# Table words of several target sets or edge units taken by one register load in a graph network kernel

## The chip, the cores and the metric

The kernel runs on one core of a Trainium2 chip. The metric is the device time of one execution in microseconds; of several runs the median counts.

## The reference, cut to what matters

There are 3125 nodes with 128 features and 100000 edges, sorted by target. Four graph layers follow each other, each with a residual sum and a layer norm: an edge MLP with batch norm, a two-way graph convolution, a residual network of four steps, and attention over the edges.

```python
edge_index = jnp.stack([src, dst])
x = _layernorm(x + _L0_gnn_ref(x, edge_index, ...), axis=-1)
x = _layernorm(x + _L1_gnn_ref(x, edge_index, ...), axis=-1)
x = _layernorm(x + _L2_gnn_ref(x, edge_index, ..., 4), axis=-1)
x = _layernorm(x + _L3_gnn_ref(x, edge_index, ...), axis=-1)

def _L0_gnn_ref(x, edge_index, W1, b1, g1, be1, W2, b2, g2, be2):
    edge_features = jnp.concatenate([x[src], x[dst]], axis=1)
    h = jax.nn.relu(_batchnorm(edge_features @ W1.T + b1, g1, be1))
    edge_updates = jax.nn.relu(_batchnorm(h @ W2.T + b2, g2, be2))
    return jax.ops.segment_sum(edge_updates, dst, num_segments=x.shape[0])
```

The other three layers need, for every pair of nodes, how many edges join them: the kernel counts that first, in a matrix, and then works with the matrix in place of the edges.

## The kernel before, in words

All five engines run their own instruction streams, written out by hand, and meet at the ends of stages. Three stages are of interest here.

**Counting (79 to 840 us).** The padded 3200 nodes are cut into NWIN = 100 sets of WN = 32 targets. The edges are taken in pairs of 128, 392 in all (NPAIR). A set's edges lie in a run of pairs, from `first` to `end`, at least two of them; neighbours may share a pair. For each pair VectorE (`one_hots`, L1392 on) makes two one-hot tiles of the sources (L1397) and one of the targets (L1399), in one of eight slots (PAIRS); TensorE (`count_pair`) multiplies them into PSUM (L1752), with four matmuls. A set ends with a matmul on zeros (L1791) that tells the others. Each engine loops on its own over the sets, VectorE in groups of four (`count_four`), TensorE in groups of twelve (GROUP, `count_group`), and for each set it needs three numbers: `first`, `end` and `before`, which with a pair's number gives its place in the run of all visits and so its slot and semaphore value. They come from a table in SBUF, `block_tab`, made by VectorE in the preparation (L1353 to L1365); row 3 holds first and end in one word, row 2 `before`. `window` (L393) reads them by `value_load`, one load per word, each with an assertion on its bounds. `before` is loaded only for the first set of a group; otherwise it is worked out in registers from the set ahead (L401). In this stage GpSimd gathers rows of a table for the first pass by indirect DMAs (L823), held back by the counts of VectorE (`one_ready`) and later by the ends of sets (`window_done`); ScalarE takes the counts out of PSUM and stores them.

**First pass over the edges (975 to 1515 us).** 98 units (NU) of 1024 edges. TensorE (`layer1`) adds the gathered source rows (L1886) and, for each block of 128 target nodes that the unit touches, a product with a one-hot tile (L1892) made by VectorE (`pass1`, L1506); then follows `layer2`, two f32 matmuls (L1905). Three of four units' rows come through DRAM (`a_in`), the fourth is gathered straight into SBUF (`a_direct`).

**Second pass (1515 to 2045 us).** The same units again. `layer2_rows` recomputes the second layer: two matmuls for the shift (L1938), 16 in f32 (L1940). ScalarE (`relu2`, L1109) and VectorE (`low_part`, L1539) take the high and low part; VectorE makes one-hot rows (L1549); `sum_edges` multiplies them, 16 matmuls per visit of a block (L1953), ScalarE (`take_sums`, L1120) takes the sum out and GpSimd (`add_sums`, L905) adds it to the node's sum. TensorE's loop takes two units per round: rows(i,0), sums of unit 2i-1, rows(i,1), sums of unit 2i.

In both passes the numbers of a unit come by `unit` (L383): one load (L386) of one packed word of `unit_tab`, with its bounds step and assertion, and then masks and shifts (L388). On each engine the load stands directly ahead of the loop over the unit's blocks.

The numbers are register values of an engine's sequencer, which also waits for semaphores, works out addresses and hands instructions to its engine.

Of the kernel before, what the change touches and what calls it, by code (L numbers as in the profile page):

```python
# [21 lines left out]
P = 128  # L22
N = 3125
NB = -(-N // P)
# [7 lines left out]
NU = EP // UE  # L32
PE_EDGES = 256
NPAIR = EP // PE_EDGES
WP = 98
WN = 32
NWIN = NP // WN
# [49 lines left out]
PAIR0 = 512  # L87
VISIT0 = 64
PAIRS = 8
SETS = 3  # L90
GROUP = 12
# [10 lines left out]
def gnn(nc, ins, out):  # L102
# [28 lines left out]
    with ctx:  # L131
# [53 lines left out]
        unit_tab = sb("unit_tab", [1, 4, NU], i32)  # L185
        block_tab = sb("block_tab", [1, 4, NWIN], i32)
        parts_tab = sb("parts_tab", [1, 8], i32)
# [4 lines left out]
        weff = sb("weff", [P, P], f32)  # L192
        wtmp = sb("wtmp", [P, 4, P], f32)
        squares = sb("squares", [P, 2 * P], f32)
# [187 lines left out]

        def unit(eng, g):  # L383


            word = eng.value_load(unit_tab[0:1, 3, ds(g, 1)], min_val=0, max_val=(VISIT0 + NB * NU) * 1024)  # L386
            def number(value, least, most):
                return nc.s_assert_within(eng.snap(value), least, most)  # L388

            return (number(word & 31, 0, NB - 1), number((word >> 5) & 31, 1, NB),  # L390
                    number(word >> 10, 0, VISIT0 + NB * NU))

        def window(eng, w, done_pairs):  # L393
# [384 lines left out]
        def _(pool):  # L778
# [113 lines left out]
            for n in range(4, 7):  # L892
                stage_start("pool", pool)
                if n == 4:

                    pool.wait_ge(S["bn2_ready"], 1)
                    pool.sem_inc(S["agg_added"], VISIT0)

                    def add_sums(i):
                        for s in range(2):  # L900
                            first, end, before = unit(pool, 2 * i + s)
# [28 lines left out]
        def _(act):  # L930
# [182 lines left out]

            def take_sums(i, s):

                first, end, before = unit(act, 2 * i + s)
# [7 lines left out]
            relu2(0, 1)  # L1124
            take_sums(0, 0)
            with act.Fori(1, NU // 2 - 1) as i:
                relu2(i, 0)
                take_sums(i + -1, 1)
                relu2(i, 1)
                take_sums(i, 0)  # L1130
            relu2(NU // 2 - 1, 0, False)
            take_sums(NU // 2 - 2, 1)
            relu2(NU // 2 - 1, 1, False)
            take_sums(NU // 2 - 1, 0)
            take_sums(NU // 2 - 1, 1)
            norm_act(act)
# [115 lines left out]
        def _(dve):  # L1252
            v = nc.vector

            def do(i):
                stepped("dve", dve, i)
# [148 lines left out]
            def count_four(i):  # L1405
                done_pairs = None
                for q in range(4):
                    w = 4 * i + q
                    first, end, before = window(dve, w, done_pairs)
# [87 lines left out]

            def pass1(j, q):
                i = 2 * j + q
                for s in range(2):  # L1500
                    g = 2 * i + s
                    first, end, before = unit(dve, g)
# [12 lines left out]
            dve.sem_inc(S["visit_ready"], VISIT0)  # L1515
            pass1(0, 0)
            with dve.Fori(0, NU // 4) as j:
                pass1(j, 1)
                pass1(j + 1, 0)
            count(NU - 2, NU - 2, 0)  # L1520
# [20 lines left out]

            def one_hot_rows(i, s):

                g = 2 * i + s
                first, end, before = unit(dve, g)
                low_part(i, s)
# [7 lines left out]

            def pass2(i):
                for s in range(2):
                    one_hot_rows(i, s)

            pass2(0)
            with dve.Fori(1, NU // 2) as i:  # L1560
                pass2(i)
            first, end, before = unit(dve, NU - 1)
            dve.wait_ge(S["agg_added"], before + end)
# [162 lines left out]
        def _(pe):  # L1726
# [49 lines left out]
            def count_group(g, ms):  # L1776
                done_pairs = None
                for m in ms:
                    w = GROUP * g + m
                    known = isinstance(w, int)  # L1780
                    first, end, before = window(pe, w, done_pairs)
                    done_pairs = before + end
# [88 lines left out]

            def layer1(j, q, s, odd=0):
# [4 lines left out]
                first, end, before = unit(pe, 2 * i + s)  # L1877
                after(pe, S["r1_made"], 2 * i + s - 1)
# [29 lines left out]

            layer1(0, 0, 0)
            layer1(0, 0, 1)  # L1910
            layer2(0, 0)
            assert NU // 4 % AHEAD == 0
            with pe.Fori(0, NU // 4 // AHEAD) as jj:
                for odd in range(AHEAD):
                    j = AHEAD * jj + odd
                    for q in (1, 0):
                        i = 2 * j + (2 - q)
                        layer1(j + (1 - q), q, 0, odd)
                        layer2(i + -1, 1)
                        layer1(j + (1 - q), q, 1, odd)  # L1920
                        layer2(i, 0)
# [21 lines left out]

            def sum_edges(i, s):

                first, end, before = unit(pe, 2 * i + s)
                hold("pe", pe, S["low_ready"], 2 * i + s + 1)
# [14 lines left out]
            layer2_rows(0, 1)  # L1962
            sum_edges(0, 0)
# [5 lines left out]
            sum_edges(NU // 2 - 1, 1)  # L1969
            pe.wait_ge(S["dve_features"], 2)  # L1970
# [253 lines left out]
```

## Time and profile before, and how to read them

| | |
|---|---|
| median of 3 runs | 4250.56 us (4240.57 to 4261.32) |
| span of the profiled execution, first to last instruction | 4243.9 us |
| median less span | 6.7 us |
| PE busy | 3447.9 us, 81% |
| DVE busy | 2654.4 us, 63% |
| ACT busy | 1496.2 us, 35% |
| POOL busy | 1050.2 us, 25% |

The profiled execution has no time of its own beside its span. PE is the matmul engine, PEld its weight loads, DVE VectorE, ACT ScalarE, POOL GpSimd, SP SyncE. An engine's name with a q (DVEq, PEldq) marks instructions of its sequencer, which don't count as busy; PE's stand under PEldq. Idle time before an instruction is put down to the one whose semaphore released it, or to "issue" where nothing visible was waited for.

### The profile page before, as it was taken

The numbers are of one execution on the slowest core, as the hardware profiler recorded it, in microseconds if no ns is written. First come the engines' busy times: TensorE is split into PE (matmuls) and PEld (weight loads), VectorE is DVE, ScalarE is ACT, GpSimd is POOL, SyncE is SP. The second block draws the span as 40 slices with busy tenths as digits, with TensorE's granted clock in tenths as the row PEclk, the third lists the DMA queues.
The fourth block names the chain that finished last, engine by engine and source line by source line (L and its number), as shares of the span: only waits on it lengthen the run. The fifth ranks groups of instructions, "written<-read, shape, count | busy, mean of one in ns | idle before, by whom it ended". The sixth has DMA issues, their size and how long they took to land. (4 is left out here: it accounts for less than half of the span.)

```text
span 4243.9 us, 85956 instructions
## 1 busy us (share of the span) xinstructions
PE 3447.9 (81%) x20439; PEld 1689.6 (40%) x20548; DVE 2654.4 (63%) x3759; ACT 1496.2 (35%) x2093; POOL 1050.2 (25%) x1132
## 2 busy tenths in 40 slices
PE   3777767686677978888898998599889989989996
PEld 1333333243344556666645554233322233332223
DVE  6877766522233455554202223699989989989995
ACT  2134555601122222222202111221088851208883
POOL 3877774665555412221000001000010000000000
PEclk8989999978898999999899999799999999999998
DMA  2255665667787866666583774511054331103333
GB/s 62 93 168 196 213 224 193 222 248 255 240 276 253 304 214 200 179 175 171 187 276 130 246 257 143 148 61 54 23 140 132 115 116 54 62 16 128 117 123 73
DMA packets 373635, 688.38 MB, mean 162 GB/s; under 512 B 136131, under 2 KB 223297, under 8 KB 372769
## 3 DMA queue, kind: packets, MB, share of 16 engines
q1 hardware_dynamic: 236400, 361.19, 26.8%
q10 hardware_dynamic: 112052, 274.54, 18.8%
q0 software_dynamic: 25088, 51.43, 4.8%
q8 instruction: 54, 0.88, 0.1%
q14 instruction: 41, 0.34, 0.0%
HBM read 453.91 MB, written 208.37 MB: 156 GB/s over the span
## 5 line engine op out<-in xcount | busy, mean ns | idle before, releaser
L823 POOL DMA_INDIRECT gat<-a_table,gidx x592 | 674.3, 1139 | 259.3 <-issue 142.5
L1703 DVE SCALAR_TENSOR_TENSOR pw<-ex,c_full 128x1564 f32<-128x1564 f32 x400 | 680.8, 1779 | 35.6 <-ACT ex L1231 30.9
L1231 ACT ACTIVATE ex<-psum 128x782 f32<-128x782 f32 x800 | 610.4, 826 | 77.4 <-PE psum L2114 58.9
L1665 DVE CUSTOM_DVE_ANT_0 masked<-psum,masks 128x1784 bf16<-128x1784 f32 x320 | 551.7, 1784 | 64.8 <-ACT masks L1204 43.7
L1752 PE MATMUL psum<-one_src,one_dst 128*128 x1968 | 417.7, 351 | 208.9 <-DVE one_dst L1399 127.6
L1397 DVE TENSOR_SCALAR one_src<-iota_sub,src_low 128x800 f16 x984 | 382.6, 430 | 191.7 <-PE psum L1752 124.7
L2123 PE MATMUL psum<-pw,vaug 128*32 128x391 f32 x3200 | 348.6, 508 | 30.2 <-DVE pw L1703 10.0
L1752 PEld LDWEIGHTS psum<-one_src,one_dst 128*128 x1968 | 189.4, 100 | 422.9 <-issue 340.4
L1539 DVE SCALAR_TENSOR_TENSOR u<-psum,u 128x1024 f16<-128x1024 f32 x98 | 120.0, 1225 | 254.8 <-ACT u L1109 254.8
L1204 ACT ACTIVATE masks<-masks,far 128x3128 bf16<-128x3128 bf16 x40 | 115.5, 2900 | 423.4 <-DMA masks<-ct_parts 423.4
L1067 ACT ACTIVATE r<-psum,vec 128x1024 f32<-128x1024 f32 x98 | 118.0, 1205 | 398.7 <-PE psum L1898 331.4
L1399 DVE SCALAR_TENSOR_TENSOR one_dst<-row_c,window_at,iota_row 128x256 f16 x492 | 234.2, 476 | 0.0
L823 POOL DMA_INDIRECT a_direct<-a_table,gidx x192 | 184.4, 961 | 166.0 <-DMA a_direct<-a_table,gidx 98.5
L2079 PE MATMUL psum<-qp,kp 96*128 96x446 bf16 (+1 forms) x700 | 172.8, 364 | 60.8 <-DVE mx L1665 31.0
L905 POOL TENSOR_TENSOR y<-y,visit_sum 128x128 f32 x122 | 105.2, 862 | 455.5 <-ACT visit_sum L1120 455.5
L1940 PE MATMUL psum<-w2s,r_in 128*128 128x128 f32 x1568 | 217.6, 296 | 0.0
L1940 PEld LDWEIGHTS psum<-w2s,r_in 128*128 128x128 f32 x1568 | 198.0, 205 | 44.2 <-issue 44.2
L1953 PE MATMUL psum<-u,ohd 128*128 128x128 f16 x1952 | 147.7, 227 | 71.6 <-issue 35.5
L1506 DVE TENSOR_SCALAR oht<-dst_bc,nodec 128x1024 f16 x122 | 60.7, 498 | 224.4 <-PE psum L1892 123.8
L1905 PE MATMUL psum<-r,W2T 128*128 128x512 f32 x392 | 198.9, 631 | 0.0
L1494 DVE BATCH_NORM_STATS2 stats<-psum 128x512 f32 (+1 forms) x196 | 126.5, 687 | 108.0 <-PE psum L1905 107.8
L2084 PE MATMUL psum<-qp,kp 96*128 96x448 bf16 x800 | 189.4, 360 | 0.0
(357 smaller groups left out, 4792.0 us busy)
## 6 DMA issues: line engine op xcount, KB each, us to landing
c_full<-c_whole SPq DMA_DIRECT2D x80, 977.5 KB, 5.0
r_edges<-r ACTq DMA_DIRECT2D x98, 512.0 KB
r_in<-r_edges ACTq DMA_DIRECT2D x98, 512.0 KB, 3.7
c_ring<-ct_parts SPq DMA_DIRECT2D x100, 480.0 KB, 4.4
c_whole<-c_sum ACTq DMA_DIRECT2D x100, 400.0 KB
a_edges<-gat SPq DMA_DIRECT2D x148, 256.0 KB, 2.6
a_in<-a_edges ACTq DMA_DIRECT2D x74, 512.0 KB, 5.6
c_ring<-ct_parts SPq DMA_DIRECT2D x100, 320.0 KB, 3.6
```

What stands on the lines that cost most here:

```text
L823: g.indirect_dma_start(to, None, a_table, bass.IndirectOffsetOnAxis(ap=gidx[:, s, k:k + 1], axis=0)).then_inc(landed, 16)
L1231: a.activation(ex[:, step_slot(n // 2), (n % 2) * 2 * CW:(n % 2 + 1) * 2 * CW].rearrange("p (h t) -> p h t", h=2), psum[:, o:o + 2 * BANK] ...
L1397: v.tensor_scalar(one_src[:, ds(slot, 1), t, 0:SUB].rearrange("p o n -> p (o n)"), iota_sub[:, :], src_low[:, ds(p * 2 + t, 1)], None, ALU ...
L1399: v.scalar_tensor_tensor(one_dst[:, ds(slot, 1), :, :].rearrange("p o t n -> p (o t) n"), row_c[:, ds(p * 2, 2)].rearrange("p (t o) -> p t ...
L1665: v.tensor_tensor_reduce(out=masked[:, n % 2, 0:count * width].rearrange("p (c t) -> p c t", c=count), in0=psum[:, first * BANK:(first + c ...
L1703: v.scalar_tensor_tensor(pw[:, step_slot(k), :].rearrange("p (h t) -> p h t", h=HQ), ex[:, step_slot(k), :].rearrange("p (h t) -> p h t", ...
L1752: last = t.matmul(bank(2 * k + half, n), one_dst[:, ds(slot, 1), s, :].rearrange("p o n -> p (o n)"), one_src[:, ds(slot, 1), s, half * HA ...
L1905: last = t.matmul(bank(4 + 2 * s + half), W["W2T"][:, :], r1[:, s, half * GE:(half + 1) * GE], start=True, stop=True)
L1940: last = t.matmul(psum[:, s * UE + k * P:s * UE + (k + 1) * P], r1_in[:, s, k * P:(k + 1) * P], w2s[:, :], start=False, stop=True, skip_gr ...
L2079: last = t.matmul(bank(first + c, width), kp[0:KQK, n // 2, ds(b * P, P)], query(quad, n // 2)[0:KQK, c0 + c * width:c0 + (c + 1) * width] ...
L2084: t.matmul(bank(7, 448), kp[0:KQK, n // 2, 0:P], query(quad, n // 2)[0:KQK, 0:448], start=True, stop=True)
L2123: last = t.matmul(psum[hh * HW:(hh + 1) * HW, 6 * BANK:6 * BANK + CW], vaug[:, k, quad * HQ + hh, :], pw[:, step_slot(k), hh * CW:(hh + 1) ...
```

## The change

Words of several sets or units are read by one load on each engine. In the counting a new table `quad_tab` has a row of five words for each group of four sets: `before` of the first set and the packed first and end of each. In the passes 2 to 4 neighbouring words of `unit_tab` are read at once. Where the load now stands differs: at the head of the loop's round, ahead of `layer2_rows`, `relu2` or `layer1`, in place of behind them. TensorE now loads `before` for the first of every four sets, ahead only for the first of a group of twelve.

```diff
-        block_tab = sb("block_tab", [1, 4, NWIN], i32)
+        block_tab = sb("block_tab", [1, 3, NWIN], i32)
+        quad_tab = sb("quad_tab", [1, NWIN // 4, 5], i32)
...
-        wtmp = sb("wtmp", [P, 4, P], f32)
+        wtmp = sb("wtmp", [P, 2, P], f32)
...
-        def unit(eng, g):
-            word = eng.value_load(unit_tab[0:1, 3, ds(g, 1)], min_val=0, max_val=(VISIT0 + NB * NU) * 1024)
+        def unit_words(eng, g, n):
+            return nc.values_load_multi_w_load_instructions(
+                unit_tab[0:1, 3, ds(g, n)], engines=[eng.engine], min_val=0, max_val=(VISIT0 + NB * NU) * 1024)[1]
+        def unit(eng, word):
...
-        def window(eng, w, done_pairs):
-            word = eng.value_load(block_tab[0:1, 3, ds(w, 1)], min_val=0, max_val=NPAIR * 512 + NPAIR)
+        def quad_words(eng, i):
+            return nc.values_load_multi_w_load_instructions(
+                quad_tab[0:1, ds(i, 1), :].rearrange("p o n -> p (o n)"), engines=[eng.engine],
+                min_val=0, max_val=NPAIR * 512 + NPAIR)[1]
+        def window(eng, words, q, done_pairs):
+            word = words[1 + q]
             first = nc.s_assert_within(eng.snap(word & 511), 0, NPAIR - 2)
             end = nc.s_assert_within(eng.snap(word >> 9), 2, NPAIR)
-            if done_pairs is None:
-                before = eng.value_load(block_tab[0:1, 2, ds(w, 1)], min_val=PAIR0 - NPAIR, max_val=PAIR0 + NWIN * NPAIR)
-            else:
-                before = nc.s_assert_within(eng.snap((done_pairs - first) & 65535), PAIR0 - NPAIR, PAIR0 + NWIN * NPAIR)
+            before = words[0] if q == 0 else (done_pairs - first) & 65535
+            before = nc.s_assert_within(eng.snap(before), PAIR0 - NPAIR, PAIR0 + NWIN * NPAIR)
...
-            do(v.scalar_tensor_tensor(block_tab[:, 3, :], block_tab[:, 1, :], 512.0, block_tab[:, 0, :], ALU.mult, ALU.add))
+            by_quad = block_tab[:, :, :].rearrange("p a (g q) -> p a g q", q=4)
+            do(v.scalar_tensor_tensor(quad_tab[:, :, 1:5], by_quad[:, 1, :, :], 512.0, by_quad[:, 0, :, :], ALU.mult, ALU.add))
+            do(v.tensor_copy(quad_tab[:, :, 0:1], by_quad[:, 2, :, 0:1]))
...
             def count_four(i):
                 done_pairs = None
+                words = quad_words(dve, i)
...
             with pe.Fori(1, NU // 2) as i:
+                words = unit_words(pe, 2 * i + -1, 2)
                 layer2_rows(i, 0)
-                sum_edges(i + -1, 1)
+                sum_edges(i + -1, 1, words[0])
                 layer2_rows(i, 1)
-                sum_edges(i, 0)
+                sum_edges(i, 0, words[1])
```

The first pass is alike with four words per round on TensorE and VectorE; in the second VectorE and GpSimd load two words at the head of a pair of units, ScalarE two words ahead of `relu2`.

## Rows read from the trace of the kernel before

**Rows 1.** Busy us (and instructions) of each engine in the stages; PEclk is the granted clock.
```profile
core 0: us, PE busy (x) PEld busy (x) DVE busy (x) ACT busy (x) POOL busy (x), PEclk, DMA share, GB/s
79.00:840.00 761.00, 549.98 (x2656) 247.96 (x2656) 551.43 (x1478) 333.94 (x593) 547.42 (x544) 0.92 0.53 181
...
1515.00:2045.00 530.00, 433.18 (x3851) 339.21 (x3850) 265.84 (x224) 135.14 (x225) 105.15 (x122) 0.94 0.65 189
```
**Rows 2.** Who waited for whom, 79 to 840 us: total us, times, longest.
```profile
PE psum L1752 <- DVE one_dst L1399: 127.6, 97, 3.3
DVE one_src L1397 <- PE psum L1752: 124.7, 96, 2.7
PE psum L1752 <- issue: 77.4, 95, 3.1
POOL gidx L820 <- PE psum L1791: 66.2, 10, 22.1
```
**Rows 3.** TensorE's timeline, 576 to 583 us: start, us, instruction, idle before.
```profile
578.76 1.51 PE L1752 MATMUL psum<-one_src,one_dst 128*128 x4 [2.45 <-issue]
```
**Rows 4.** PE's sequencer, 576.1 to 578.8 us: ns min/median/max, first and last start.
```profile
L395 PEldq FUSED_REGOPS  x2: 46/102/157, 576.2 to 577.0; - x2
L395 PEldq TENSOR_LOAD <-block_tab x1: 682/682/682, 576.3 to 576.3; - x1
L395 PEldq SEQ_ASSERT  x1: 18/18/18, 577.2 to 577.2; - x1
...
L1752 PEldq ALU_OP  x1: 32/32/32, 578.5 to 578.5; - x1
```
**Rows 5.** The loads of line 395 on both engines, 79 to 560 us.
```profile
L395 DVEq TENSOR_LOAD <-block_tab x54: 300/311/1003, 80.0 to 558.4; - x54
...
L395 PEldq TENSOR_LOAD <-block_tab x52: 297/306/693, 79.8 to 557.9; - x52
```
**Rows 6.** First pass: a line of the waits, and GpSimd's last gathers.
```profile
PE psum L1886 <- DMA a_direct<-a_table,gidx: 103.2, 17, 23.1
...
L823 POOL DMA_INDIRECT a_direct<-a_table,gidx x37: 941/947/1094, 1399.5 to 1477.8; - x37
```
**Rows 7.** Who waited for whom in the second pass, 1525 to 2040 us.
```profile
DVE u L1539 <- ACT u L1109: 254.8, 98, 11.0
...
PE psum L1953 <- issue: 35.5, 73, 2.9
PE psum L1953 <- ACT visit_sum L1120: 26.4, 24, 1.7
PE psum L1938 <- issue: 19.2, 44, 0.5
```
**Rows 8.** TensorE's timeline, one round of the second pass.
```profile
1700.35 0.60 PE L1938 MATMUL psum<-row,onesb 3*128 3x512 bf16 x2 [0.43 <-issue]
1700.88 2.05 PE L1940 MATMUL psum<-w2s,r_in 128*128 128x128 f32 x16
1703.31 1.19 PE L1953 MATMUL psum<-u,ohd 128*128 128x128 f16 x16 [0.38 <-issue]
```
**Rows 9.** Line 386 on PE: 1700.5 to 1703.3 us, then its loads in the second pass.
```profile
L386 PEldq FUSED_REGOPS  x2: 69/121/173, 1700.9 to 1701.4; - x2
...
L386 PEldq TENSOR_LOAD <-unit_tab x98: 297/302/1582, 1524.7 to 2033.5; - x98
```
**Rows 10.** PE's table loads of the counting, then those after 700 us.
```profile
L395 PEldq TENSOR_LOAD <-block_tab x100: 297/308/1002, 79.8 to 830.8; - x100
...
L399 PEldq TENSOR_LOAD <-block_tab x9: 307/309/609, 81.2 to 819.0; - x9
...
L395 PEldq TENSOR_LOAD <-block_tab x24: 298/602/1002, 704.5 to 830.8; - x24
```
**Rows 11.** Working out `before` on PE (400 to 840 us), and the table's last step on DVE.
```profile
L401 PEldq FUSED_REGOPS  x134: 57/102/146, 400.6 to 832.6; - x134
L401 PEldq ALU_OP  x67: 36/36/36, 400.7 to 832.5; - x67
...
L1365 DVE SCALAR_TENSOR_TENSOR block_tab<-block_tab x1: 251/251/251, 71.3 to 71.3; 1x100 int32<-1x100 int32 x1
```

More of the change, by code:

```diff
@@ L899, in add_sums @@
                     def add_sums(i):
+                        words = unit_words(pool, 2 * i, 2)
                         for s in range(2):
-                            first, end, before = unit(pool, 2 * i + s)
+                            first, end, before = unit(pool, words[s])
                             with pool.Fori(first, end) as b:
@@ L1112, in relu2, with take_sums @@
                     fetch_r1(i + 1, s)
-            def take_sums(i, s):
-                first, end, before = unit(act, 2 * i + s)
+            def take_sums(word):
+                first, end, before = unit(act, word)
                 with act.Fori(first, end) as b:
@@ L1124, in _ @@
             relu2(0, 1)
-            take_sums(0, 0)
+            take_sums(unit_words(act, 0, 1)[0])
             with act.Fori(1, NU // 2 - 1) as i:
+                words = unit_words(act, 2 * i + -1, 2)
                 relu2(i, 0)
-                take_sums(i + -1, 1)
+                take_sums(words[0])
                 relu2(i, 1)
-                take_sums(i, 0)
+                take_sums(words[1])
+            words = unit_words(act, NU - 3, 3)
             relu2(NU // 2 - 1, 0, False)
-            take_sums(NU // 2 - 2, 1)
+            take_sums(words[0])
             relu2(NU // 2 - 1, 1, False)
-            take_sums(NU // 2 - 1, 0)
-            take_sums(NU // 2 - 1, 1)
+            take_sums(words[1])
+            take_sums(words[2])
             norm_act(act)
@@ L1406, in count_four @@
                 done_pairs = None
+                words = quad_words(dve, i)
                 for q in range(4):
                     w = 4 * i + q
-                    first, end, before = window(dve, w, done_pairs)
+                    first, end, before = window(dve, words, q, done_pairs)
                     done_pairs = before + end
@@ L1496, in count, with pass1 @@
                 i.then_inc(h2_taken[3], 1)
-            def pass1(j, q):
+            def pass1(j, q, words):
                 i = 2 * j + q
@@ L1501, in pass1 @@
                     g = 2 * i + s
-                    first, end, before = unit(dve, g)
+                    first, end, before = unit(dve, words[s])
                     hold("dve", dve, dst_loaded[2 * q + s], 16 * j + 16)
@@ L1515, in _ @@
             dve.sem_inc(S["visit_ready"], VISIT0)
-            pass1(0, 0)
+            pass1(0, 0, unit_words(dve, 0, 2))
             with dve.Fori(0, NU // 4) as j:
-                pass1(j, 1)
-                pass1(j + 1, 0)
+                words = unit_words(dve, 4 * j + 2, 4)
+                pass1(j, 1, words[0:2])
+                pass1(j + 1, 0, words[2:4])
             count(NU - 2, NU - 2, 0)
@@ L1540, in low_part, with one_hot_rows @@
                                        0.0, u[:, s, :, 0, :], ALU.max, ALU.subtract).then_inc(S["low_ready"], 1)
-            def one_hot_rows(i, s):
+            def one_hot_rows(i, s, word):
                 g = 2 * i + s
-                first, end, before = unit(dve, g)
+                first, end, before = unit(dve, word)
                 low_part(i, s)
@@ L1555, in pass2 @@
             def pass2(i):
+                words = unit_words(dve, 2 * i, 2)
                 for s in range(2):
-                    one_hot_rows(i, s)
+                    one_hot_rows(i, s, words[s])
             pass2(0)
@@ L1561, in _ @@
                 pass2(i)
-            first, end, before = unit(dve, NU - 1)
+            first, end, before = unit(dve, unit_words(dve, NU - 1, 1)[0])
             dve.wait_ge(S["agg_added"], before + end)
@@ L1780, in count_group @@
                     known = isinstance(w, int)
-                    first, end, before = window(pe, w, done_pairs)
+                    if m % 4 == 0:
+                        words = quad_words(pe, (GROUP // 4) * g + m // 4)
+                    first, end, before = window(pe, words, m % 4, done_pairs)
                     done_pairs = before + end
@@ L1870, in _, with layer1 @@
             pe.sem_inc(S["visit_free"], VISIT0 + 2)
-            def layer1(j, q, s, odd=0):
+            def layer1(j, q, s, word, odd=0):
                 i = 2 * j + q
@@ L1876, in layer1 @@
                     "p (k m f) -> p k m f", m=2, f=P)
-                first, end, before = unit(pe, 2 * i + s)
+                first, end, before = unit(pe, word)
                 after(pe, S["r1_made"], 2 * i + s - 1)
@@ L1907, in layer2 @@
                 last.then_inc(h2_psum[3], 1)
-            layer1(0, 0, 0)
-            layer1(0, 0, 1)
+            words = unit_words(pe, 0, 2)
+            layer1(0, 0, 0, words[0])
+            layer1(0, 0, 1, words[1])
             layer2(0, 0)
@@ L1915, in _ @@
                     j = AHEAD * jj + odd
+                    words = unit_words(pe, 4 * j + 2, 4)
                     for q in (1, 0):
                         i = 2 * j + (2 - q)
-                        layer1(j + (1 - q), q, 0, odd)
+                        layer1(j + (1 - q), q, 0, words[2 * (1 - q)], odd)
                         layer2(i + -1, 1)
-                        layer1(j + (1 - q), q, 1, odd)
+                        layer1(j + (1 - q), q, 1, words[2 * (1 - q) + 1], odd)
                         layer2(i, 0)
@@ L1942, in layer2_rows, with sum_edges @@
                 last.then_inc(h2_psum[4], 1)
-            def sum_edges(i, s):
-                first, end, before = unit(pe, 2 * i + s)
+            def sum_edges(i, s, word):
+                first, end, before = unit(pe, word)
                 hold("pe", pe, S["low_ready"], 2 * i + s + 1)
@@ L1962, in _ @@
             layer2_rows(0, 1)
-            sum_edges(0, 0)
+            sum_edges(0, 0, unit_words(pe, 0, 1)[0])
             with pe.Fori(1, NU // 2) as i:
+                words = unit_words(pe, 2 * i + -1, 2)
                 layer2_rows(i, 0)
-                sum_edges(i + -1, 1)
+                sum_edges(i + -1, 1, words[0])
                 layer2_rows(i, 1)
-                sum_edges(i, 0)
-            sum_edges(NU // 2 - 1, 1)
+                sum_edges(i, 0, words[1])
+            sum_edges(NU // 2 - 1, 1, unit_words(pe, NU - 1, 1)[0])
             pe.wait_ge(S["dve_features"], 2)
```

## The prediction

> **What bounds the kernel now.** I began with the busy time by stage [rows 1], since the change touches three stretches only: the counting of edge pairs (79 to 840 us), the first pass over the edges (975 to 1515) and the second (1515 to 2045). What follows, up to 4244 us, holds no table load and stays as it is.
>
> In the counting stage neither TensorE nor VectorE is busy over 75%, and the waits view blames both sides: PE stands idle 127.6 us "for" DVE, 77.4 us for nothing visible, and DVE 124.7 us for PE [rows 2]. The timeline breaks the tie. PE stands still 2.45 us before the first matmul of a set of targets [rows 3]; its sequencer is at work all that time, on steps that start every 0.1 us or so: an address step, the load of 0.68 us, a bounds step of 0.16 us and its assertion, then masks, shifts and more assertions up to the wait for the one-hots at 578.5 [rows 4]. Nor is DVE late: by 560 us it has loaded 54 sets' words where PE has loaded 52 [rows 5], so PE has about two sets of one-hots in hand, and an idle put down to DVE only names a releaser that had long been done. So here PE's own sequencer sets the pace, and each us it saves is a us of the stage, until DVE becomes the bound; DVE's 124.7 us of waiting for PE is the room for that.
>
> The first pass is another case. PE waits 103.2 us for rows gathered straight into SBUF, the last of which GpSimd issues at 1477.8 us, close to the stage's end [rows 6]. The gather sets the pace there.
>
> In the second pass PE is idle before the first product of a unit (35.5 us, 73 times, "issue") and at the head of the loop (19.2 us, 44 times); for another engine, ScalarE, it waits 26.4 us [rows 7]. ACT and DVE wait for it. The timeline of one round of the loop [rows 8] shows 0.43 us of idle at the head and 0.38 us before the products. Again the sequencer: while 16 f32 matmuls run (2.05 us) it works through a unit's load and numbers and comes out late [rows 9].
>
> **Costs, part by part.** Durations are of one execution with a span of 4243.9 us; the median of the runs shown is 4250.6, so 6.7 us lie around the span or are scatter. I take the change off the median.
>
> *Counting stage, PE.* Loads fall from 109 (100 words, 9 "before" words [rows 10]) to 25. Each that goes takes along an address step of 0.046 us and two gaps between sequencer steps of about 0.06 us: 0.166 us, worked out from the starts and lengths in [rows 4]. 84 x 0.166 = 13.9 us. The loads' own time: a median of about 0.31 us up to 700 us [rows 5, 10] and of 0.602 us for the last 24 of 100 [rows 10], 0.38 us on average. 84 x 0.38 = 31.9 us. (Medians leave out a tail up to 1.0 us, which would add; the stretches at the lower granted clock, where TensorE is behind its sequencer, would take away. I let these two cancel.) Against that, 100 words are now fetched as the 2nd to 5th of a load. **What such a further word costs no row shows**, since every load of this kernel has one word. Lower bound: nothing, as the load is one instruction. Upper bound: a whole load, 0.38 us. I take 0.26 us: the shortest load is 0.297 us [rows 10], a plain register operation 0.036 us [rows 11], and I hold the difference to be one trip to the table, paid per word. That is nearer to the upper row, because the only thing seen to cost time in a load is the trip. 100 x 0.26 = 26.0 us. Bounds checks: 16 more words are checked (0.157 + 0.018 + two gaps = 0.30 us each, 4.7 us), 25 "before" words get a second check (about 0.29 us, 7.2 us), and PE no longer works out "before" for 16 sets (0.50 us each from [rows 11], 8.0 us): 3.9 us on top. Stage: 13.9 + 31.9 - 26.0 - 3.9 = **15.9 us gained**; 42 us if further words are free, 4 us if each costs a load.
>
> *Counting stage, DVE.* 125 loads (100 and one more for each group) become 25 with the same 125 words. It saves the same kind of time and so stays ahead of PE. The words of four sets are checked in one lump at the head of a group, some 1.5 to 2 us later than now; the one-hots in hand (about two sets, at 7.6 us a set on average) cover that. If that cover were gone, DVE's lump would cost 25 x 2 us.
>
> *What waits behind the stage.* GpSimd's gather is held to the counts: its index copies waited 66.2 us, in 10 waits, for ends of sets [rows 2], so an earlier count lets it go on earlier, and its remaining run, up to the last gather at 1477.8 us [rows 6], moves as a whole.
>
> *First pass.* 4 loads become one of four words on PE and DVE. PE has 103.2 us of waiting to hide a loss, and no gain can show: 0 us, between -3 and +3. The cover is the wait for gathered rows; without it the lump at the loop's head (3 further words and 4 checks, about 2 us, 25 times) would lie behind the f32 matmuls of layer 2.
>
> *Second pass, PE.* 98 loads become 50. Each of the 48 takes along 0.069 + 0.302 + two gaps = 0.49 us [rows 9]: 23.5 us; 48 further words at 0.26 us give back 12.5 us. The checks are as many as before. But they move: load and both checks now stand at the loop's head, where PE is already idle, and leave the place behind the f32 matmuls. Moved work costs nothing as long as the sequencer is the bound at both places, for then only its sum counts: before the products it would now be some 0.5 us early, and that lead is carried to the head. Where the granted clock is at its lower level (0.94 on average [rows 1], so one unit in eight or so) the old place was covered and the new one is not; I take 2 us off. 23.5 - 12.5 - 2 = **9 us gained**; 21 us with free words, 5 us at a full load each (0.302 us). ACT, POOL and DVE wait for PE there (DVE 254.8 us for ACT's result [rows 7]), so their own lumps are covered.
>
> *Preparation.* One more small DVE instruction on the table, like the 0.251 us one that it follows [rows 11], 0.3 us with its step.
>
> Sum: -15.9 - 9 + 0.3 = -24.6 us, 4250.6 - 24.6 = **4226.0 us**, 0.6% less. What a measurement of this kernel can tell from no change is about 0.5%, 21 us, so the forecast lies just beyond it.
>
> The Trainium skill has a rule against the change. "Runtime: NRT & Kernel Launch", section "Instruction fetch mechanics", says that a register load costs about 200 ns per register even in bulk. By that, and with the rest of my sum, the time would be about 4217 us (an estimate from that page). The trace agrees in kind with a shortest load of 297 ns for one register, but shows no bulk load.
>
> **Rivals.**
>
> 1. *Further words are free.* The load is fetched as one piece. For it: it is one instruction with one operand. Against: nothing in the trace. -42 - 21 + 0.3 gives 4188 us; the tail left out of the medians could make it 4180.
>
> 2. *Each word costs a whole load* of 0.38 or 0.30 us, contention included; late in the counting stage loads double to 0.602 us, which may be waiting at the memory and would then be paid per word. -4 - 5 gives 4242 us.
>
> 3. *The gather does not follow.* GpSimd is busy 547 of 761 us in the counting stage [rows 1] and its chain of landings then runs the first pass. If it can't go faster, the 15.9 us are lost in longer waits for gathered rows, and 9 us are left: 4242 us. Against it stand the 66.2 us that it waited for the sets.
>
> 4. *Slower: the head of the second pass.* If the lead gained before the products cannot be carried through them (16 matmuls take 1.19 us there [rows 8], which may be the sequencer's own rate), PE gains at most its 35.5 us of idle but pays at the head 48 x (0.49 + 0.26 + 2 x 0.295) = 64 us: 29 us lost, against 16 gained in the counting: 4263 us, and 4276 us with rival 2's price. It decides from the point where the saving before the products is worth less than 48 of those 64 us. Against: the lead needs no faster array, only a queue, and the queue holds at least the 16 f32 matmuls: the sequencer starts on the unit's numbers at 1700.9 us with all of them handed over, and they run until 1702.9 [rows 8, 9].
>
> **Chances.** Forecast 0.45; free words 0.18; full price 0.14; gather 0.15; slower 0.08. Free words lie wholly beyond the 21 us, of the forecast's own spread (4215 to 4235) about two thirds, of the others nearly nothing: faster 0.50. Slower by over 21 us only when rival 4 comes with dear words: 0.06. Same: 0.44. The range goes from 4183, most of free words, to 4256, which takes in rivals 2 and 3 and scatter; it leaves out the tail of free words and most of rival 4.
>
> **What would show it.** On PE, table loads drop from 109 to 25 in the counting and from 98 to 50 in the second pass. The decisive row is the median of the five-word loads: 1.3 us by the forecast, 0.3 by free words, 1.8 at full price; of the two-word loads 0.56, 0.3 or 0.6. The last set's count should end 16 us earlier, the first pass 16 us earlier with PE's wait for gathered rows still near 103 us, and the second pass should be 9 us shorter, with idle before the products near zero and about 1.3 us at each head. I am wrong if DVE, not PE's sequencer, ends the idle at the sets' starts, if the wait for gathered rows grows by what the counting gained, or if the second pass gets longer.

## The result: 1.0% slower, and the profile after

The changed kernel takes 4294.55 us (median of 4 runs, 4289.59 to 4296.22) against 4247.89 us before: a ratio of 1.0104, 95% interval 1.0084 to 1.0123. The forecast was 4226, its range 4183 to 4256. The profiled execution has a span of 4294.5 us, 50.6 more than before.

The stages of the changed kernel, in the columns of [rows 1]:

```profile
79.00:840.00 761.00, 546.05 (x2663) 247.39 (x2664) 545.58 (x1477) 333.87 (x596) 582.80 (x550) 0.91 0.54 182
1515.00:2045.00 530.00, 427.67 (x3554) 357.83 (x3553) 250.95 (x205) 125.16 (x204) 80.95 (x112) 0.84 0.57 165
```

The line to look at is the second, for the second pass. TensorE completed some 300 fewer matmuls in the same 530 us than in [rows 1], and its granted clock is 0.84 in place of 0.94. The products' matmuls of the counting (L1752, now L1770), the first pass (L1892, now L1912) and the second pass (L1953, now L1975) follow, before and then after; "83.9 to 837.9" gives the starts of the first and the last in us:

```profile
L1752 PE MATMUL psum<-one_src,one_dst x1968: 329/333/542, 83.9 to 837.9; 128*128 x197
L1892 PE MATMUL psum<-oht,b_parts x430: 379/379/634, 986.2 to 1496.4; 128*128 x144
L1953 PE MATMUL psum<-u,ohd x1952: 219/227/314, 1527.9 to 2037.8; 128*128 128x128 f16 x196
```
```profile
L1770 PE MATMUL psum<-one_src,one_dst x1968: 329/333/542, 84.3 to 832.7; 128*128 x197
L1912 PE MATMUL psum<-oht,b_parts x430: 379/379/634, 982.8 to 1491.4; 128*128 x144
L1975 PE MATMUL psum<-u,ohd x1952: 219/219/315, 1522.8 to 2082.4; 128*128 128x128 f16 x196
```

The counting ends 5.2 us earlier, the first pass 5.0 us earlier. From its first product to its last the second pass takes 559.6 us in place of 509.9, a loss of 49.7 us. It ends 44.6 us later; the other 6 us of the 50.6 lie behind it, where nothing was changed and where the profiles of this case scatter (2206 to 2212 us from the last product to the end). Loads of the tables in the changed kernel, those of the counting on both engines and then PE's in the second pass:

```profile
L401 PEldq TENSOR_LOAD <-quad_tab x25: 593/1512/2954, 79.0 to 812.4; - x25
L401 DVEq TENSOR_LOAD <-quad_tab x25: 597/1217/2342, 79.2 to 802.2; - x25
...
L387 PEldq TENSOR_LOAD <-unit_tab x50: 309/536/1675, 1519.8 to 2079.1; - x50
```

A five-word load takes 1.5 us on PE by its median, a two-word load 0.54 us; in [rows 9, 10] one word took 0.30 or 0.31. The forecast had named 1.3 and 0.56 us. PE's waits in the second pass (1525 to 2120 us) answer to [rows 7]:

```profile
PE psum L1960 <- DVE u L1556: 47.5, 27, 1.8
PE psum L1960 <- issue: 36.6, 21, 2.9
PE psum L1975 <- ACT visit_sum L1131: 20.4, 24, 1.2
...
PE psum L1975 <- issue: 2.4, 1, 2.4
```

The idle before the products (now line 1975) has gone as forecast, 35.5 us to 2.4. The idle at the loop's head (line 1960) has grown from 19.2 to 84.1 us, 1.75 us in each of 48 rounds. Half of it is put down to DVE's u, which is the releaser named and not the cause, as in the counting before: where nothing was waited for ("issue"), the gap is as long, 1.74 us on average against 1.76. TensorE's timeline of one round shows what follows, to be held against [rows 8]:

```profile
1755.95 1.17 PE L1975 MATMUL psum<-u,ohd 128*128 128x128 f16 x16 [0.43 <-DVE ohd L1566]
...
1759.00 1.03 PE L1960 MATMUL psum<-row,onesb 3*128 3x512 bf16 x2 [1.75 <-issue]
1759.96 3.78 PE L1962 MATMUL psum<-w2s,r_in 128*128 128x128 f32 x16
1763.53 1.88 PE L1975 MATMUL psum<-u,ohd 128*128 128x128 f16 x16
...
1765.88 2.05 PE L1962 MATMUL psum<-w2s,r_in 128*128 128x128 f32 x16
```

Behind a head with 1.75 us of idle the 16 f32 matmuls take 3.78 us, and half a round later the same 16 take 2.05. 3.78 is 1.84 times 2.05: that is the lower of the two clock levels, 1.2 in place of 2.4 GHz. In [rows 8], behind 0.43 us of idle, the first group takes 2.05 as well. The round of the changed kernel above is one of the worst. Of the 44 groups behind a head that the trace shows whole, 10 take 3.78 us or nearly so, 7 take 2.05 and the rest lie between; their mean is 2.94 us. Of the 48 in the middle of a round all but one take 2.05. Before, the mean behind a head was 2.25 us.

So the theory for the experiments was **A: the moved load makes a longer idle at the head of TensorE's loop, and TensorE's clock falls to its lower level for the first part of most rounds**. Rivals were the lumps of loads at the loop heads of the other engines (B) and the two-word load itself (C).

### The profile page after: what moved, and what is told of

Same layout as the page of the kernel before. It is cut to its first block and busy times, and to the rows that moved or that the text cites. A ratio compares the mean times of both kernels' runs of the same rounds, so it can differ in the third digit from the quotient of the medians.

```text
span 4294.5 us, 85040 instructions
## 1 busy us (share of the span) xinstructions
PE 3473.0 (81%) x20439; PEld 1738.2 (40%) x20548; DVE 2657.4 (62%) x3760; ACT 1493.4 (35%) x2093; POOL 1059.7 (25%) x1132
## 5 line engine op out<-in xcount | busy, mean ns | idle before, releaser
L833 POOL DMA_INDIRECT gat<-a_table,gidx x592 | 707.1, 1194 | 264.5 <-issue 148.0
L1683 DVE CUSTOM_DVE_ANT_0 masked<-psum,masks 128x1784 bf16<-128x1784 f32 x320 | 552.5, 1784 | 64.4 <-ACT masks L1217 43.4
L1770 PE MATMUL psum<-one_src,one_dst 128*128 x1968 | 418.1, 352 | 210.7 <-DVE one_dst L1414 132.2
L1770 PEld LDWEIGHTS psum<-one_src,one_dst 128*128 x1968 | 188.6, 100 | 419.9 <-issue 336.9
L1962 PE MATMUL psum<-w2s,r_in 128*128 128x128 f32 x1568 | 248.1, 323 | 0.0
L1962 PEld LDWEIGHTS psum<-w2s,r_in 128*128 128x128 f32 x1568 | 225.1, 228 | 48.6 <-issue 48.6
L1120 ACT ACTIVATE u<-psum 128x1024 f16<-128x1024 f32 x98 | 100.3, 1023 | 349.4 <-PE psum L1962 349.4
L916 POOL TENSOR_TENSOR y<-y,visit_sum 128x128 f32 x122 | 85.5, 701 | 522.1 <-ACT visit_sum L1131 522.1
L1975 PE MATMUL psum<-u,ohd 128*128 128x128 f16 x1952 | 161.7, 246 | 28.0 <-ACT visit_sum L1131 20.4
```

The lines of the kernel that those rows point to most:

```text
L833: g.indirect_dma_start(to, None, a_table, bass.IndirectOffsetOnAxis(ap=gidx[:, s, k:k + 1], axis=0)).then_inc(landed, 16)
L1683: v.tensor_tensor_reduce(out=masked[:, n % 2, 0:count * width].rearrange("p (c t) -> p c t", c=count), in0=psum[:, first * BANK:(first + c ...
L1770: last = t.matmul(bank(2 * k + half, n), one_dst[:, ds(slot, 1), s, :].rearrange("p o n -> p (o n)"), one_src[:, ds(slot, 1), s, half * HA ...
L1962: last = t.matmul(psum[:, s * UE + k * P:s * UE + (k + 1) * P], r1_in[:, s, k * P:(k + 1) * P], w2s[:, :], start=False, stop=True, skip_gr ...
```

## The experiments

All times are device medians; the ratio stands against the kernel before, run on the same chip beside it.

### Undoing TensorE's part of the second pass

```diff
-                words = unit_words(pe, 2 * i + -1, 2)
                 layer2_rows(i, 0)
-                sum_edges(i + -1, 1, words[0])
+                sum_edges(i + -1, 1, unit_words(pe, 2 * i + -1, 1)[0])
                 layer2_rows(i, 1)
-                sum_edges(i, 0, words[1])
+                sum_edges(i, 0, unit_words(pe, 2 * i, 1)[0])
```

> The changed kernel, but TensorE loads one word per unit in the second pass, ahead of the products, as it did before. Theory A (TensorE's idle at the loop's head lowers its granted clock): the second pass is back near 511 us from 560, the granted clock in it near 0.94 from 0.84, and the whole near 4245 us. Rival B (the lumps of ScalarE, VectorE and GpSimd at their loops' heads make the loss): the second pass stays at 555 to 560 us and the whole at 4290 to 4295. If both share, something between.

Measured: 4226.99 us, ratio 0.9956 (0.9941 to 0.9970). The second pass lasts from 1521.3 to 2016.8 us, 495.5 us. This is the changed kernel with one of its parts taken out, and it is 67.6 us faster than the changed kernel and faster than the one before, by 23 us of the medians, from 13 to 25 by the interval. Rival B falls: the other engines' lumps were all still there. The loss comes from TensorE's part, and the granted clock of 1515 to 2045 us is back at 0.95. Delay and clock went together, so this run does not yet say which of them cost the time. The second pass is also some 15 us shorter than theory A had it; the run of ScalarE's part below shows where most of that comes from.

### TensorE's part of the second pass alone

TensorE's two-word load at the head of the loop, put into the kernel before, with nothing else of the change.

> The kernel before with one part of the change: TensorE's two-word load at the head of the second pass's loop. Theory A: the second pass takes 560 us where it took 511, clock near 0.84, the whole about 4298 us. Rival B: nothing changes, 4248 us. The other stages are those of before in both.

Measured: 4330.57 us, ratio 1.0196 (1.0161 to 1.0230), 81 us slower; the second pass takes 597.2 us (1523.1 to 2120.3). That is 32 us more than A said, and the granted clock of 1515 to 2045 us is 0.81. With this part in place the rest of the change is worth 36 us (4330.57 less 4294.55), without it 23 us (4249.72 less 4226.99). PE's waits show where some of it lies; the wait for ScalarE's copies, 20.4 us in the changed kernel, is 37.5 us here:

```profile
PE psum L1949 <- DVE u L1550: 46.0, 26, 1.8
PE psum L1949 <- issue: 38.2, 21, 3.5
PE psum L1964 <- ACT visit_sum L1131: 37.5, 24, 2.2
```

### The same load, one line further down

```diff
-                words = unit_words(pe, 2 * i + -1, 2)
                 layer2_rows(i, 0)
+                words = unit_words(pe, 2 * i + -1, 2)
```

> The changed kernel with TensorE's two-word load of the second pass moved by one line: behind the first layer2_rows of the round, whose f32 matmuls run meanwhile, in place of ahead of it. The same instructions are executed. Theory A (place decides, by the idle at the head and the clock): the second pass takes 500 to 515 us, the clock near 0.94, the whole 4235 to 4250. Rival C (a two-word load itself is what costs, wherever it stands): 4290 to 4295.

Measured: 4231.46 us, ratio 0.9964 (0.9949 to 0.9980), second pass 492.2 us (1525.9 to 2018.1). The sequencer executes the same instructions; only the place has changed, and 63 us go; the granted clock between 1540 and 2000 us is 0.97. Rival C falls. Against one load per unit (4226.99) there is no difference beyond scatter, so the two-word load gains nothing visible on TensorE, even where it is covered. PE's waits:

```profile
PE psum L1975 <- issue: 42.8, 38, 2.6
PE psum L1975 <- ACT visit_sum L1131: 21.5, 23, 1.2
PE psum L1960 <- issue: 20.0, 47, 0.5
```

The idle at the head is back at 20.0 us. Before the products it is now 42.8 us in 38 places in place of 35.5 in 73: probably because the first unit of a round carries both words and checks.

### Idle alone, in two doses

Three and eight semaphore increments at the head of the loop in the kernel before; no load is touched. Nobody waits for the semaphore.

```diff
             with pe.Fori(1, NU // 2) as i:
+                for _ in range(8):
+                    pe.sem_inc(S["idle_steps"], 1)
                 layer2_rows(i, 0)
```

> The kernel before with three semaphore increments, on a semaphore that nobody reads, at the head of TensorE's loop in the second pass: some 0.35 us of further idle in 48 rounds and nothing else. A delay alone adds 48 x 0.35 = 17 us: 4267 us, clock in the second pass as before (0.95). If idle of 0.8 us in a round already lowers the granted clock, 4280 us or more and a clock of 0.90 or less.

> The same with eight increments: some 0.95 us more at each head, 1.4 us of idle in all, near the 1.8 us of the changed kernel. A delay alone adds 46 us: 4296 us, clock 0.95. By the theory that idle at the head lowers the clock, more than that: 4310 to 4335 us, clock 0.82 to 0.88, with no load touched at all.

Measured: 4277.77 us with three (ratio 1.0082, 1.0056 to 1.0108) and 4343.51 us with eight (1.0235, 1.0217 to 1.0253). PE's waits with three and then with eight, the head being line 1938:

```profile
PE psum L1938 <- DVE u L1539: 24.5, 28, 0.9
PE psum L1938 <- issue: 17.2, 20, 0.9
```
```profile
PE psum L1938 <- issue: 46.0, 30, 1.7
PE psum L1938 <- DVE u L1539: 29.5, 18, 1.7
```

Idle per head is 41.7/48 = 0.87 us and 75.5/48 = 1.57 us. Between 1540 and 2000 us the granted clock (the third number from the end of each row) reads as follows, for the kernel before, for three, for eight, and for the changed kernel:

```profile
1540.00:2000.00 460.00, 381.44 (x3439) 298.12 (x3439) 235.82 (x197) 120.75 (x198) 95.29 (x110) 0.96 0.63 182
```
```profile
1540.00:2000.00 460.00, 368.64 (x3237) 293.23 (x3236) 223.82 (x187) 114.48 (x187) 88.77 (x102) 0.93 0.60 174
```
```profile
1540.00:2000.00 460.00, 358.70 (x2883) 290.52 (x2883) 197.88 (x166) 101.83 (x166) 80.72 (x91) 0.86 0.54 157
```
```profile
1540.00:2000.00 460.00, 373.15 (x3096) 313.75 (x3094) 218.34 (x179) 109.75 (x178) 71.80 (x97) 0.83 0.57 166
```

With eight, the second pass grows by 88 us (1528.6 to 2126.5 against 509.9 before). The head's idle grew by 75.5 - 19.7 = 56 us; some 32 us more are lost elsewhere, at a clock of 0.86. With three it grows by 31 us, 22 of them at the head, the clock at 0.93. So the loss is there without any load, and in both doses it is larger than the idle added at the head. The run with eight lay above the range named for it (4310 to 4335 us). The three-increment run lay just below the 4280 us named for a clock loss, and its clock of 0.93 between the two cases named; it leaves open whether 0.87 us of idle already costs clock.

A longer idle at the head does not lower the clock each time. Two stretches of the run with eight, both with about 1.66 us of idle at nearly every head:

```profile
1560.00:1600.00 40.00, 30.45 (x277) 23.60 (x277) 17.87 (x17) 10.28 (x16) 7.75 (x8) 1.00 0.61 183
1680.00:1720.00 40.00, 31.53 (x226) 25.85 (x226) 15.80 (x14) 7.89 (x14) 6.47 (x8) 0.74 0.44 130
```

Up to 1630 us all f32 groups take 2.05 us and a round lasts 10 to 11 us; the first group of 3.78 us starts at 1636.37. What sets off the first fall is not shown.

### A busy array, the same delay

Seven spare matmuls on zeros ahead of the load at the head of the changed kernel's loop. They do no part of the computation.

```diff
             with pe.Fori(1, NU // 2) as i:
+                for _ in range(7):
+                    t.matmul(bank(6), zerosb[:, 0:P], zerosb[:, :], start=True, stop=True)
                 words = unit_words(pe, 2 * i + -1, 2)
```

> The changed kernel with seven spare matmuls on zeros (512 columns each, into a bank that holds nothing) at the head of TensorE's loop in the second pass, ahead of the load, so that the array is busy while its sequencer loads. The useful work starts no earlier than in the changed kernel. If the delay at the head is the loss, it stays at 4294 us or gets worse. If the lower clock that follows the idle is the loss, the clock is back near 0.95 and the whole at 4235 to 4260 us. The spare matmuls do no part of the computation.

Measured: 4246.62 us, ratio 0.9999 (0.9983 to 1.0015). Timeline, and the clock between 1540 and 2000 us:

```profile
1754.70 1.17 PE L1975 MATMUL psum<-u,ohd 128*128 128x128 f16 x16 [0.41 <-DVE ohd L1566]
...
1756.32 1.67 PE L1988 MATMUL psum<-zerosb 128*128 128x512 bf16 x7 [0.32 <-issue]
1757.92 0.60 PE L1960 MATMUL psum<-row,onesb 3*128 3x512 bf16 x2
1758.45 2.05 PE L1962 MATMUL psum<-w2s,r_in 128*128 128x128 f32 x16
```
```profile
1540.00:2000.00 460.00, 413.00 (x3680) 307.08 (x3680) 240.88 (x197) 118.94 (x195) 73.96 (x109) 0.99 0.63 182
```

This run splits the loss. From the start of the products to the next useful matmul it takes 1757.92 - 1754.70 = 3.22 us here and 1759.00 - 1755.95 = 3.05 us in the changed kernel; over all rounds with full-speed products the means are 3.21 and 2.97. So the useful work starts no earlier than in the changed kernel. Yet the clock is 0.99, the f32 matmuls take 2.05 us, and the second pass lasts 515.5 us (1522.9 to 2038.4) where it took 559.6. **44 us of the loss were clock**, given back by work that computes nothing (48 us by the medians of the whole). The other 23 us to the 492.2 of the covered load are the delay itself. The waits agree: against the covered load the changed kernel idles 84.1 - 20.0 = 64.1 us more at the heads and 42.8 - 2.4 = 40.4 us less before the products, 23.7 us in all. The split is good to some us, as the clock here is a little above the 0.97 of the covered load and the delay a little longer than in the changed kernel.

The Trainium skill, "TensorE: Matmul & The Clock Gate", section "HAM oscillation — how this bites in real kernels", describes a clock that falls again and again where bursts of matmuls alternate with waits. The changed kernel's timeline, 3.78 and 2.05 us in turn, agrees in kind; the waits of the page's case last about 3 to 5 us, these 1.75 us.

### Rows of eight words in the counting's table

```diff
-        quad_tab = sb("quad_tab", [1, NWIN // 4, 5], i32)
+        quad_tab = sb("quad_tab", [1, NWIN // 4, 8], i32)
...
-                quad_tab[0:1, ds(i, 1), :].rearrange("p o n -> p (o n)"), engines=[eng.engine],
+                quad_tab[0:1, ds(i, 1), 0:5].rearrange("p o n -> p (o n)"), engines=[eng.engine],
```

The reason was a pattern in the changed kernel's loads. The fourth and fifth of PE's 25, at a quiet time:

```profile
L401 PEldq TENSOR_LOAD <-quad_tab x1: 1242/1242/1242, 271.2 to 271.2; - x1
L401 PEldq TENSOR_LOAD <-quad_tab x1: 609/609/609, 306.5 to 306.5; - x1
```

A row of five words is 20 bytes long, so only each fourth row starts at a multiple of 16 bytes, as the fifth load's does. On PE the seven loads of such rows took 0.59 to 0.98 us, the other 18 took 1.23 to 2.95 us.

> The changed kernel with rows of eight words in the table of the counting in place of five, so that each group's five words start at a multiple of 32 bytes; in the changed kernel only every fourth load, which starts at a multiple of 16, took 0.6 us, the others 1.2 us or more. Theory T (words from a start that is a multiple of 16 bytes come four at a time, otherwise one at a time): nearly all loads have a minimum of 0.6 us and the counting ends 10 to 20 us earlier, the whole at 4275 to 4285 us; less if TensorE then waits longer for ScalarE's low parts. Rival F (the fourth loads are short for another reason, such as their place in TensorE's loop): nothing changes, 4294 us.

Measured: 4274.52 us, 20 us less than the changed kernel by the medians, 16 us by the ratios (against before: 1.0066, 1.0040 to 1.0091). The counting's last matmul starts at 808.2 us in place of 832.7, in a profiled execution that was the fastest of its six, at 4259.82 us. Its loads:

```profile
L401 PEldq TENSOR_LOAD <-quad_tab x25: 583/685/1654, 79.7 to 788.4; - x25
L401 DVEq TENSOR_LOAD <-quad_tab x25: 585/827/1489, 79.9 to 777.6; - x25
```

Five words from such a start take 0.59 us at least; from other starts 1.23 to 1.25 at quiet times, which is 0.94 us for four further words over the 0.30 of one, 0.23 us each. Rival F falls: the start of the row decides. That words come four at a time from such a start, as theory T has it, fits (0.59 us is twice 0.30) but is not shown by itself. The Trainium skill gives about 200 ns per register even in bulk ("Runtime: NRT & Kernel Launch", "Instruction fetch mechanics"): that agrees with loads from other starts (0.23 us) and not with these (0.07 us a further word). And the gain of the counting does reach the later stages: the first pass, too, starts its last matmul 28.7 us earlier than in the changed kernel (1462.7 against 1491.4).

### Only ScalarE's part

```diff
-                relu2(i, 0)
-                take_sums(i + -1, 1)
+                words = unit_words(act, 2 * i + -1, 2)
+                relu2(i, 0)
+                take_sums(words[0])
```

> The kernel before, and of the change only ScalarE's part in the second pass: its two-word load ahead of relu2 in place of a load per unit between relu2 and take_sums. In the run with TensorE's second pass as before, TensorE's 14 us of waiting for ScalarE to have taken a sum (19 waits) had shrunk to 1.5 us and the second pass by 14 us. Theory S (ScalarE's load stood in the way of its copies): that wait goes and the whole is near 4236 us (4230 to 4241). Rival: the 14 us came from VectorE's or GpSimd's loads or from the clock of single runs, and here the time stays within 3 us of 4248.

Measured: 4236.00 us, ratio 0.9972 (0.9959 to 0.9984), second pass 489.0 us (1531.9 to 2020.9). By the medians 13 us are gained, from 7 to 17 by the interval. The profiled second pass is 20.9 us shorter than before, but its clock between 1540 and 2000 us reads 0.99 against 0.96, so part of that is not the move. PE's waits:

```profile
PE psum L1966 <- issue: 40.2, 84, 3.3
PE psum L1951 <- issue: 19.0, 43, 0.5
PE psum L1966 <- ACT visit_sum L1131: 15.3, 23, 1.1
```

The wait for ScalarE's copy is 15.3 us in place of the 26.4 of [rows 7]: it did not go, as theory S had it, but most of its waits fell from 1.1 to 1.2 us to 0.65 each. (In the run with TensorE's second pass as before it is 15.9 us, in 24 waits; the expectation's 14 and 1.5 us are not what the waits show.) Before the change ScalarE loaded a unit's word between `relu2` and `take_sums`, while TensorE stood before the second product of a unit and waited for the copy of the first.

### Only the counting's part

The kernel before with `quad_tab` and nothing else of the change.

> The kernel before, and of the change only the counting: the table with rows of five words and one load per four sets on VectorE and TensorE. Theory W (one trip per word from most starts, and a new wait of TensorE for ScalarE's low parts, some 20 us, that eats most of the rest): the counting ends 5 to 8 us earlier and the whole is 4240 to 4244 us. Rival: the counting's part is worth the forecast 16 us or more, and the whole is 4232 or less.

Measured: 4238.47 us, ratio 0.9980 (0.9965 to 0.9995), 11 us less by the medians, from 2 to 15 us by the interval: more than theory W said, less than the forecast. In the profiled execution the counting's last matmul starts at 834.7 us, 3.2 us earlier, where W had 5 to 8. PE's waits in the counting have a long one, the third, that was 3.0 us before:

```profile
PE psum L1761 <- DVE one_dst L1407: 130.8, 85, 5.5
PE psum L1761 <- issue: 57.7, 96, 5.0
PE psum L1761 <- ACT c_lo L988: 22.4, 19, 1.9
```

### Both mends together

TensorE's load of the second pass one line down, and rows of eight words.

> Both mends of the changed kernel at once: TensorE's two-word load behind the first layer2_rows, and rows of eight words in the counting's table. The one gave 63 us on the changed kernel, the other 20; they lie in different stages, so if they only add the whole is 4294.6 - 63 - 20 = 4211 us (4203 to 4220). If the earlier end of the counting is lost again because gathers do not follow, it is near 4231.

Measured: 4215.38 us, ratio 0.9933 (0.9916 to 0.9951). The two add up to within 5 us of the 4211 expected. This version beats both kernels: 33 us less than before (4248.24 us beside it; 21 to 36 by the interval), 79 less than the changed one.

## Why the prediction was wrong

**The step that failed** is "Moved work costs nothing as long as the sequencer is the bound at both places, for then only its sum counts", and with it the "9 us gained" of the second pass; it was a loss of 49.7 us. The sum of the sequencer's steps did not count alone. In the shadow of the f32 matmuls (2.05 us [rows 8]) they were nearly free; at the head, with the array empty, they were idle time, and idle time there mostly took the clock down. Against the covered load the loss is 67 us: 44 of clock, by the filled head, and 23 of uncovered delay. Against the kernel before it is 49.7, since ScalarE's part gained in the same stage. The lead that was to be "carried to the head" did not arrive. The idle before the products is gone, but the head stood idle for 1.75 us, where the forecast had "about 1.3 us"; by the prediction's own prices, 0.43 us of idle before, a load of 0.49, a further word of 0.26 and two checks of 0.295 make 1.77 us, with no lead at all. Why it did not arrive is open. The sign named for the forecast did not fit its own sum either: 48 heads with 1.3 us are 62 us of idle, against 54.7 us at both places before, which is no gain of 9 us.

**The clock** did appear in the working, but only as a condition of the place ("I take 2 us off"), never as something that the change itself sets. Rival 4 named the right place and the right sign and had the delay nearly right: 64 us paid at the heads and at most 35.5 gained before the products, 29 us lost. Against the kernel before the waits show 84.1 - 19.7 = 64.4 us paid and 35.5 - 2.4 = 33.1 gained, 31 us lost. It lacked the clock, and got a chance of 0.08. Without the moved line the rest of the change comes to 4226.99 us. That this is the forecast within 1 us is chance, as the terms show:

- *Counting: 15.9 us forecast, 5.2 us in the profile of the changed kernel, 11 us in the runs of its part alone.* Two terms were off. The 0.26 us for each further word held in kind, 0.23 us at quiet times; but the median five-word load was 1.51 us, not 1.3, since loads grew to 2 us and more later in the stage. That is what rival 2 said in part. (Its price for the second pass, "5 us at a full load each", should read 7 by the prediction's own terms, 23.5 - 14.5 - 2, and its total 4240.) And a wait was missed: PE now waits 22.4 us for ScalarE's low parts (3.0 us before), probably since the sets within a group follow each other faster and the low part of one must be out before its bank is used again. PE's "issue" idle fell by as much in the counting's part alone (77.4 to 57.7 us) as this wait grew. That it is what ate the gain was only read from the profiles, not tried. VectorE's own lump at the head of a group, which the prediction held to be covered, may have a part: the longest idle put down to its one-hots grew from 3.3 to 5.5 us.
- *That the gather follows an earlier count* held: with rows of eight words the first pass ended 28.7 us earlier than in the changed kernel behind a counting 24.5 us shorter, and with both mends 22.6 us earlier behind one 21.0 us shorter. Rival 3 falls. PE's wait for gathered rows was 89.4 us in the changed kernel and 98.9 with both mends, against 103.2. The smaller step of the change itself, 5.0 behind 5.2 us, is within what single profiles scatter.
- *First pass, 0 us*: held, within what a profile tells; PE waited 9 us more for VectorE's one-hot tiles (14.0 us against 5.3), under the cover of the gather.
- *ScalarE's load "covered"* was wrong the other way: its move was worth 13 us. "ACT, POOL and DVE wait for PE there" was read from the totals, but in units with two visits PE waits for ACT, the 26.4 us of [rows 7], and the load stood in that path.
- *Further words free* (rival 1, 0.18): wrong for these addresses (0.23 us a word), though for starts at multiples of 16 bytes nearly so (0.07).

## What to carry to other kernels

Before a scalar load or other sequencer work is hoisted, see what the engine's array does meanwhile: behind a queue of long matmuls the work was nearly free here, at the head of a loop with an empty queue it was idle time, and the clock came on top. In this kernel that came to 44 us of clock on 23 us of delay with 1.75 us of idle at each head, and to some 32 us lost elsewhere on 56 us of added idle with 1.57 us. So read the granted clock of the stage beside the idle time. A load of several table words gained more here when its row started at a multiple of 16 bytes; pad the rows. And an engine that waits most of the time can still stand in the path of a few visits: look at who waits for it, not only for whom it waits.

## What the runs showed of the hardware that was not expected

- TensorE's clock fell and rose within most rounds of 11 to 12 us (f32 groups of up to 3.78 us and of 2.05 us in turn) though the idle at the heads was about 1.8 us at most, but for a single wait at the pass's end; mean granted clock 0.83 with 1.75 us of idle at each head, 0.86 with 1.57, 0.93 with 0.87, against 0.99 with spare matmuls in the gap. And it need not fall: with eight increments the first nine heads with 1.6 to 1.7 us of idle left it at its upper level.
- A register load from SBUF took 0.30 us for one word at quiet times. Five words take 0.59 us from a start at a multiple of 16 bytes and 1.24 us from others. In the changed kernel single loads of five words took up to 2.95 us between 560 and 700 us, at a DMA share of 0.67; up to 400 us, at a share of 0.39, none took more than 1.62.
- Eight semaphore increments on TensorE's sequencer, 0.051 us each by their records, added (75.5 - 19.7)/48 = 1.16 us to the idle of a round: some 0.145 us each.
